# A macaron layer (MoE FFN, attention, MoE FFN): a wait for the last batch's transposes ahead of the third batch of scatters

## The reference

```
x = x + 0.5 * ffn(layernorm(x))
x = x + attention(layernorm(x))        # 16 heads of 128, full softmax, weights as codes * scales
x = x + 0.5 * ffn(layernorm(x))
```

## Time and profile before

| what | value |
|---|---|
| median of 3 timed runs | 1044.06 us (1043.67 to 1045.27) |
| profiled execution, span | 1069.7 us |
| TensorE busy | 980.6 us (92%) |
| VectorE busy | 798.7 us (75%) |
| ScalarE busy | 676.3 us (63%) |
| GpSimd busy | 626.3 us (59%) |
| DMA moved | 183.07 MB, mean 171 GB/s |

### The profile page before, as it was taken

The page is one execution under the profiler, slowest core; times in us unless marked ns, Lnnn a source line. Parts: engine busy times, 40 slices in busy tenths (PEclk is TensorE's granted clock), DMA queues, the critical chain, the costliest instruction groups (busy, mean ns, idle before and its releaser), DMA issues. The chain is left out here.

```text
span 1069.7 us, 18752 instructions
## 1 busy us (share of the span) xinstructions
PE 980.6 (92%) x5314; PEld 844.7 (79%) x5314; DVE 798.7 (75%) x1682; ACT 676.3 (63%) x1485; POOL 626.3 (59%) x916
## 2 busy tenths in 40 slices
PE   5669999899999999999999999999999997579995
PEld 4459987677888888888888888888888885469985
DVE  7777577788887777787777877778788876358545
ACT  5545645667776777777776777767777765135641
POOL 1740458776436876767787666787536377630252
PEclk9769999999999999999999999999999999879997
DMA  9877652766456675787768877777754469966653
GB/s 313 286 254 236 199 188 69 152 152 115 79 100 142 138 128 105 188 182 182 150 142 210 216 190 159 172 149 185 162 97 80 87 146 197 391 234 197 194 177 104
DMA packets 329891, 183.07 MB, mean 171 GB/s; under 512 B 273344, under 2 KB 314944, under 8 KB 329152
## 3 DMA queue, kind: packets, MB, share of 16 engines
q1 hardware_dynamic: 323056, 155.66, 59.8%
q0 software_dynamic: 6432, 20.98, 5.9%
q10 hardware_dynamic: 304, 5.24, 1.4%
HBM read 73.31 MB, written 46.92 MB: 112 GB/s over the span
## 5 line engine op out<-in xcount | busy, mean ns | idle before, releaser
L669 POOL CAST R<-turned 128x512 fp32r<-128x512 f16 x512 | 290.5, 617 | 215.2 <-DMA turned<-work 152.4
L1703 PE MATMUL bank<-R 128*128 128x512 f32 (+2 forms) x1056 | 391.7, 371 | 25.3 <-DVE R L1343 10.0
L1704 PE MATMUL bank<-R 128*128 128x512 f32 (+2 forms) x1056 | 380.7, 360 | 0.0
L1705 PE MATMUL bank<-R 128*128 128x512 f32 (+2 forms) x1056 | 379.7, 360 | 0.0
L1703 PEld LDWEIGHTS bank<-R 128*128 128x128 f32 x1056 | 206.0, 195 | 59.5 <-issue 13.8
L1705 PEld LDWEIGHTS bank<-R 128*128 128x128 f32 x1056 | 205.7, 195 | 28.3
L1704 PEld LDWEIGHTS bank<-R 128*128 128x128 f32 x1056 | 206.2, 195 | 26.7
L975 ACT ACTIVATE bank<-bank,soft 128x512 f32<-128x512 f32 x256 | 170.3, 667 | 70.6 <-DVE soft L1515 70.6
L1508 DVE SCALAR_TENSOR_TENSOR R<-bank,bias,R 128x512 fp32r<-128x512 f32 x192 | 143.7, 749 | 68.5 <-ACT R L995 37.5
L1515 DVE TENSOR_REDUCE soft<-bank 128x1 f32<-128x512 f32 x256 | 168.6, 686 | 25.1 <-PE bank L1705 25.1
L1529 DVE SCALAR_TENSOR_TENSOR work<-bank,soft,work 128x512 f16<-128x512 f32 x256 | 185.1, 742 | 0.8 <-ACT work L988 0.8
(11 more groups left out here) (164 smaller groups left out, 1379.2 us busy)
## 6 DMA issues: line engine op xcount, KB each, us to landing
work<-in_parts SPq DMA_DIRECT2D x64, 256.0 KB, 4.1
work<-in_ffn_w SPq DMA_DIRECT2D x34, 384.0 KB, 4.8
work<-xs_dram SPq DMA_DIRECT2D x96, 128.0 KB
y_tiles<-work SPq DMA_DIRECT2D x48, 256.0 KB
w_dram<-work SPq DMA_DIRECT2D x16, 768.0 KB, 4.6
R<-w_dram SPq DMA_DIRECT2D x16, 768.0 KB
y_tiles<-in_empty ACTq DMA_DIRECT2D x2, 2176.0 KB
X<-in_x SPq DMA_DIRECT2D x4, 512.0 KB, 4.9
```

The costliest lines, as they stand in the source:

```text
L669: nc.gpsimd.tensor_copy(whole_into(m, l, kb), whole_block(m, u, l, kb)).then_inc(s["cast_pool"], 1)
L1703: nc.tensor.matmul(out, ah, bh, start=(i == 0 and first), stop=False)
L1704: nc.tensor.matmul(out, ah, bl, start=False, stop=False)
L1705: last = nc.tensor.matmul(out, al, bh, start=False, stop=(i == n - 1))
```

## The change

GpSimd waits for semaphore `xt1` at 8, that is for both halves of batch 3's transposes, after it has seen batch 2's places and before it issues batch 2's eight scatters. Nothing else is changed.

More of the change, by code:

```diff
@@ L783, in pool_program @@
     pool.wait_ge(s["pos1"], 1)
+    pool.wait_ge(s["xt1"], KT * QB)
     to_experts(1, 2, 0)
```

## The result

| | median us | lowest to highest | runs |
|---|---|---|---|
| kernel before | 1042.91 | 1041.52 to 1045.27 | 11 |
| kernel after | 1047.18 | 1044.67 to 1049.35 | 11 |

The ratio is 1.003, with the interval [1.0016, 1.0044]: slower by 3.1 us (1.7 to 4.6); the medians of the table lie 4.3 us apart, inside that interval. On the 1044.06 us of the prediction that is 1047.2 us. So the forecast of no change did not come true: what it put at 0 costs 3 us.

The account below looks back on a forecast made before the run. The prediction took the start of the second FFN's full loop over tiles as the bound. Its terms (wait, batch 2's landing, batch 3 and fill, experts) were all 0, leaving 1044.1 us, range 1039.2 to 1047.0.

Parts of the forecast that it names:

- the pause: Between the recorded end of batch 3's transposes and ScalarE's start of copying them: 6.4 us in the profile.
- The wait itself: GpSimd's added wait instruction ahead of batch 2's scatters: put at 0 to 0.3 us, taken as 0.
- Batch 3 and the fill 1.2 us later: GpSimd's queue behind batch 2: batch 3's first scatter and the fill would each move 1.2 us later.
- The fifth pair has 3 us to spare: Fifth pair of tiles, which needs batch 3 and fill: loaded 3 us early, so a 1.2 us delay is covered.
- Batch 2 lands before the table: Before SyncE's first tile load: batch 2's last scatter lands 1.4 us before the table; effect 0, up to +2.3 us.
- The experts' weights land earlier: Expert weight loads on the DMA engines: would land up to 2.5 us earlier, but nobody waits; worth 0.
- The sum: Whole kernel: wait 0, batch 2's landing 0 (up to +2.3), batch 3 and fill 0, experts 0; 1044.1 us timed.
- The scatters hold back TensorE's signals: Batch 3's transposes: holding batch 2 back frees up to 6.4 us; gain taken as 4, 1040 us; chance 0.36.
- One unbroken stream: Batches 2 and 3 scatter without a gap, holding up logits, ranks and table: taken as +3 us, 1047; chance 0.16.
- slower by landing: First tile load: batch 2 lands 0 to 2.3 us late while the expert burst fills the engines; over 2.1 us, chance 0.06.

Follow-up runs that it names:

- e0_before: The kernel before, unchanged, run and profiled a second time; ratio 0.9992 to the kernel before.
- e3: Kernel before, with only batch 3's scatters and the fill held until the table of tiles is made; ratio 1.0037.
- e5: Kernel before, with batch 3's scatters and the fill held until VectorE has written the table's column; ratio 1.0027.
- e6: Changed kernel without the last two expert weight loads (experts 10 and 11); ratio 1.0036 to the kernel before.
- e7: Kernel before without the last two expert weight loads (experts 10 and 11); ratio 0.9988.
- e4: Kernel before, with the last of batch 2's eight scatters issued behind the first two of batch 3; ratio 1.0022.
- e9: Changed kernel with the fill issued behind the first three scatters of batch 3; ratio 1.0061 to the kernel before.
- e8: Kernel before, batch 3 held until VectorE has written the table's column, fill issued behind batch 3's first three scatters; ratio 0.9993.

## What the prediction had right and what it had wrong

**What bounds the kernel.** Right: the change matters only through the start of the loop over tiles, and the full loop passes the shift on. Wrong was the picture of the chain ahead of it. The prediction saw that the first profile's span was 25.6 us above the median of the timed runs and allowed that the pause was the profile's own (that part came true), but it still took the intervals of that chain for its terms. Three intervals were shorter in e0_before: the pause, the way from ScalarE's copy to the positions, and that to the table.

**The wait itself, 0.** Nothing else of the instruction shows, but the release comes later than taken: the first scatter starts 1.18 us behind ScalarE's start (923.73 less 922.55), where the prediction had 0.34 (934.84 + 0.3, less 934.80). That is 0.8 us, outside its bound of 0.3, and it goes into both of the next steps. A part of it is a misreading: ScalarE's first copy needs only the first half of the transposes (`xt1` at 7), GpSimd's wait both (`xt1` at 8). In after (TensorE's timeline):

```profile
921.86 1.09 PE L1715 MATMUL bank<-cst,work 128*128 128x128 f32 x8 [0.36 <-ACT work L842]
```

The recorded end of both halves is 922.95, 0.4 us behind ScalarE's start, and GpSimd starts 0.8 us after that.

**Batch 3 and the fill 1.2 us later.** This step failed by size: 1.2 us forecast, 3.5 measured. In after the positions are ready at 930.06 and batch 3 starts at 933.87; with the usual 0.3 us between, 3.5 us late. The difference adds up within a tenth: from ScalarE's copy to the first scatter of batch 3 the first profile has 9.17 us (943.97 less 934.80), e0_before 7.79 (929.09 less 921.30), 1.4 less; with the 0.8 of the release it makes 1.2 + 1.4 + 0.8 = 3.4. The fill is 3.6 us later.

**The fifth pair has 3 us to spare.** Failed by size as well. Where TensorE does wait for that pair, its transposes start 3.4 to 3.6 us behind the fill's landing (e3: 955.42 less 952.0; e5: 957.00 less 953.4; e6: 952.63 less 949.1). In e0_before the fill lands at 947.1, so the pair could have been transposed at 950.6; it is at 952.16. The slack is 1.6 us. The fill's landing also takes longer: 9.1 us in after and 8.8 in e5, against 7.5 in e0_before (8.0 in the earlier trace rows). That is not a matter of its lateness alone, for in e3, with the fill later still, it is 7.0; the cause is open. A delay of 3.6 us at the issue and 1.6 us at the landing against a slack of 1.6 would leave the fifth pair 3.6 us late if the first pairs were in time; in e5, where they are, it is 3.5 (from A 40.8 against 37.4).

**Batch 2 lands before the table.** This is the step that failed, and it failed by choice: the landing was put at 2.0 us and its effect at 0, and the first load came 3.4 us past where the table would have let it (4.4 us behind the table, against 0.9). The margin was put at 3.4 us (944.0 to 947.42); it was 1.3 (932.61 to 933.95), 0.8 less for the release, 1.2 less for the chain from the copy to the table (12.6 us in the first profile, 11.4 in after). And of the two bounds for the landing, 2.0 and 6.5 us, I took the lower, because the expert burst seemed to be over at 940. In after the engines carry 378 to 426 GB/s until 936. The upper bound was about right: e0_before has a median of 5.7 us for its scatters, and 6.7, just above the bound, for batch 2's last (DMA issues from 905 to 935, and of the last one):

```profile
xs_dram<-work,pos POOLq DMA_INDIRECT x18, 5.7
...
xs_dram<-work,pos POOLq DMA_INDIRECT x1, 6.7
```

With 5.7 us behind 932.61 one is at 938.3, and the load stands at 938.31; after's trace has no landing of that scatter itself. The Trainium skill, "DMA: Bandwidth & Descriptors", section "Anatomy of one DMA — SWDGE (gpsimd) path", has the fit from which the prediction worked out its estimate of 2.3 us for 128 KB; the trace doesn't agree with it where the engines are full (5.7), and is nearer to it where they are not (3.1 at most in e6). The same section's remark on the late semaphore update is not isolated by any run here.

**The experts' weights land earlier, worth 0.** Right in effect, as e7 shows: even two experts less gain nothing that can be told.

**The sum.** Wait 0, landing 0, batch 3 and fill 0 should have read: landing 3.4 us, fill 3.5 us, and of these about the larger, not the sum: when the first pairs are late already, the fifth pair's load has that much more room, and in after TensorE doesn't wait for it. Up to the sixth pair that is 4.6 us with what the lower clock adds after the first waits, and 3.1 us in the timed runs. The gap between 4.6 and 3.1 is not resolved; the spread of single profiles, with e0_before the shortest, can hold most of it. That the two parts don't add up is shown by e4 (landing alone, 1.0022), e5 (fill alone, 1.0027) and after (both, 1.0030 [1.0016, 1.0044], where the sum would be 1.0049).

**The rivals.** "The scatters hold back TensorE's signals" fell with e0_before: scatters over the transposes, and no pause. From A to the table after has 17.9 us and e0_before 18.1; nothing is won there. "One unbroken stream" has nearly the measured number, 1047, with a wrong mechanism: the stream is unbroken (932.61, 933.87), but neither logits nor ranks nor table are held, the table even comes a little sooner. The right mechanism was "slower by landing", put at 0 to 2.3 us and given 0.06: its price was bounded by a table at 941.0 against a scatter landing at 944.1, both built on the first profile, and it knew nothing of the fill as a second one.

**The range** reached from 1039.2 to 1047.0. Counted on the prediction's 1044.06 us the change stands at 1047.2 (1045.7 to 1048.7), at the upper end; counted on the 1042.91 us of the eleven runs it stands at 1046.0, inside. That the range comes so close is luck: its upper end came from the rival of the unbroken stream at +3, whose mechanism did not occur, while the prediction's own bounds for the steps that failed give +2.3 us for the landing and nothing for the fill. Its lower end is no middle either: the middle of the gains of 2.1 to 6.4 us would be 1039.8.

## What to carry to other kernels

Before costing anything by a profile, compare its span with the timed runs; where they are 2% apart, margins of one to three microseconds read from it are not margins, and a step that rests on one needs its bound in the range. The landing of a DMA, not its issue, is what the next engine waits for, and it is to be taken under the traffic of that moment. When a stream in a queue is moved, follow it to its last member: here one scatter and the fill decided, each enough for about the whole loss, so that undoing the scatter's part alone (e6) brought nothing back.

## What the runs showed of the hardware

**A scatter takes longer to land when the engines are full.** The same 128 KB take a median of 5.7 us with the engines at 394 GB/s on average (e0_before, 905 to 935) and at most 3.1 us at 118 GB/s (e6), while GpSimd's own part is 0.96 us in both, one every 1.27 us.

**Tile loads under the fill's traffic land late.** In e9, from 942 to 947, the software queue moves 1.39 MB in 177 packets (7.9 KB each) and the hardware queue 0.28 MB in 299 (0.9 KB each): a ratio of 5 in bytes, though the small ones are more in number. Tile loads took up to 7.4 us to land; the first eight in after, all landed by 946.5, as the bulk of the fill began to move, took 2.1 to 3.2. The Trainium skill, "DMA: Bandwidth & Descriptors", section "Queues, rings and completion order", says that an engine takes turns between its queues packet by packet. In e8 the trace agrees with that: DMA queues from 940 to 943 (packets, MB, share):

```profile
q0 software_dynamic: 66, 1.08, 90.8%
q1 hardware_dynamic: 66, 0.07, 6.3%
```

As many packets of each queue, but 15 times the bytes for the software queue, whose packets here hold 16 KB. Not all of e9 fits: from 941 to 944 it has 80 packets against 1, although the loads issued at 939.7 and 940.3 were still to land; why is open.

**Behind short waits TensorE's granted clock was lower.** The waits of 1.64 and 1.81 us ahead of the first two pairs in after come behind a stretch at a granted clock of 1.00 (936 to 939) and are followed by one at 0.55, near the lower of its two levels. The second pair's transposes are 3.6 us later than in e0_before (from A 27.75 against about 24.15), the third pair's 4.5 us: the other 0.9 us come between the two pairs, for the most part in that stretch: 7.3 us from one pair to the next against 6.4. e5, with 2.98 us of waiting at the fifth pair, has 0.73 behind it. In e0_before, where TensorE doesn't wait for tiles, the same stretch is granted 1.00.
